# One kernel for cross attention and a mixture of experts: x's four transposes as one piece in the fourth step, and half of the projection moved behind the third step's transposes

## The reference

```
x = x + attention(layernorm(x), ctx)       # 32 batches, 112 rows of 256; ctx 375 rows of 192
    q = x @ Wq; k, v = ctx @ Wkv            # 16 heads of 64
    out = softmax(q k^T / 8) v @ Wproj + bproj
x = x + experts(layernorm(x))               # 8 experts, FF 512, the best 2 of each row, weighted
    hidden = silu(h @ gate_w_e) * (h @ up_w_e);  out_e = hidden @ down_w_e
```

## Time and profile before

| | |
|---|---|
| median of 3 runs | 1471.22 us (1470.12 to 1472.51) |
| the profiled execution | 1469.35 us, its span 1467.6 us |
| busy share of the span | PE 97%, PEld 86%, DVE 72%, ACT 58%, POOL 43% |
| granted clock of PE, mean | 0.994 |

### The profile page before, as it was taken

The page is one execution under the profiler, slowest core; times in us unless marked ns, Lnnn a source line. Parts: engine busy times, 40 slices in busy tenths (PEclk is TensorE's granted clock), DMA queues, the critical chain, the costliest instruction groups (busy, mean ns, idle before and its releaser), DMA issues.

```text
span 1467.6 us, 38599 instructions
## 1 busy us (share of the span) xinstructions
PE 1426.4 (97%) x11960; PEld 1264.4 (86%) x11961; DVE 1054.7 (72%) x2868; ACT 854.5 (58%) x2392; POOL 624.9 (43%) x671
## 2 busy tenths in 40 slices
PE   6999999999999999999999999999997999999996
PEld 5888889888888888888888898888886788888885
DVE  5667777777777777777777777777767776666664
ACT  5566556555665566656655656566555565555553
POOL 3634344344545343544344444545436243333332
PEclk9999999999999999999999999999999999999999
DMA  9322222222222232322222222212128243333232
GB/s 264 108 68 69 75 72 76 67 76 67 73 67 75 72 88 76 99 74 67 73 67 77 70 73 70 73 38 73 31 64 312 50 69 54 57 51 57 51 57 26
DMA packets 101508, 114.75 MB, mean 78 GB/s; under 512 B 17276, under 2 KB 88172, under 8 KB 101356
## 3 DMA queue, kind: packets, MB, share of 16 engines
q1 hardware_dynamic: 88300, 95.25, 22.3%
q0 software_dynamic: 12144, 15.66, 6.0%
q10 hardware_dynamic: 1024, 3.34, 0.7%
HBM read 62.28 MB, written 51.93 MB: 78 GB/s over the span
## 4 chain that ended last, share of the span: by engine, by line
PE 91%; DVE 3%; DMA 3%; issue 1%; ACT 0%; ACTq 0%; POOLq 0%; DVEq 0%; SPq 0%
PE bank L1486 26%; PE bank L1429 21%; PE bank L1555 11%; PE bank L1531 10%; PE bank L1521 9%; PE bank L1576 6%; PE bank L1493 4%; DMA out<-y_out,dest_now 2%; PE bank L1729 2%; DVE probT L1285 1%; PE bank L1682 1%; DVE Wgu L1138 1%; DMA WkU_whole<-in_L_xattn_Wkv 1%; DVE stat L1127 0%; DVE x L1125 0%
## 5 line engine op out<-in xcount | busy, mean ns | idle before, releaser
L891 ACT ACTIVATE prob<-bank,neg_max 112x375 f32<-112x375 f32 x512 | 300.4, 589 | 136.1 <-DVE neg_max L1279 136.1
L1279 DVE TENSOR_REDUCE neg_max<-bank 112x1 f32<-112x375 f32 x512 | 243.8, 539 | 16.4 <-PE bank L1521 16.3
L1531 PE MATMUL bank<-ident,prob 112*125 112x112 f32 x1536 | 213.8, 273 | 2.6 <-ACT prob L891 2.4
L1531 PEld LDWEIGHTS bank<-ident,prob 112*125 112x125 f32 x1536 | 198.3, 188 | 16.1 <-ACT prob L891 4.7
L1555 PEld LDWEIGHTS bank<-probT,V 125*64 125x64 f32 x3072 | 149.0, 137 | 39.7 <-issue 37.0
L822 POOL DMA_INDIRECT out<-y_out,dest_now x63 | 97.8, 1552 | 199.9 <-DMA out<-y_out,dest_now 139.8
L1046 DVE TENSOR_TENSOR K_l<-bank,K_h 128x376 fp32r<-128x376 f32 x256 | 140.3, 549 | 57.1 <-ACT K_h L847 52.7
L1555 PE MATMUL bank<-probT,V 125*64 125x112 f32 x3072 | 176.6, 264 | 3.3 <-DVE probT L1285 2.5
L1429 PE MATMUL bank<-Wgu,hT_h 128*128 x504 | 164.7, 408 | 3.4 <-DVE hT_l L1347 2.8
L845 ACT COPY V<-bank 125x512 f32<-125x512 f32 x96 | 56.4, 587 | 164.7 <-PE bank L1493 162.2
L847 ACT CAST K_h<-bank 128x376 fp32r<-128x376 f32 x256 | 121.0, 473 | 31.2 <-PE bank L1486 29.7
(11 more groups left out here) (217 smaller groups left out, 3962.1 us busy)
## 6 DMA issues: line engine op xcount, KB each, us to landing
bins<-pad_rows SPq DMA_DIRECT2D x29, 1032.0 KB, 6.0
inv_rows<-sums SPq DMA_DIRECT2D x126, 128.0 KB, 2.9
h_in<-bins SPq DMA_DIRECT2D x63, 129.0 KB, 2.2
Wgu<-in_L_ffn_gate_up_w SPq DMA_DIRECT2D x6, 1024.0 KB, 6.8
y_sb<-in_ctx SPq DMA_DIRECT2D x32, 187.5 KB, 2.7
y_sb<-in_ctx SPq DMA_DIRECT2D x62, 93.8 KB, 2.7
x_sb<-in_x SPq DMA_DIRECT2D x16, 224.0 KB, 2.9
x_res<-in_x SPq DMA_DIRECT2D x32, 112.0 KB, 2.5
```

The costliest lines, as they stand in the source:

```text
L891: nc.scalar.activation(prob[:, j, :], S_ps[j][0:LQ, 0:LKV], ACT.Exp, bias=neg_max[:, j:j + 1], accum_out=row_sum[:, head // HB, head % HB: ...
L1279: nc.vector.tensor_reduce(neg_max[:, j:j + 1], S_ps[j][0:LQ, 0:LKV], AX.X, ALU.max, negate=True).then_inc(max_done, 1)
L1531: last = nc.tensor.transpose(S_ps[j][0:KR, t * LQ:t * LQ + LQ], prob[:, j, t * KR:t * KR + KR], ident[0:LQ, 0:LQ])
```

## The change

`xT` becomes one piece of four transposes into one bank, in place "early" of the even batch's fourth step, with one copy by ACT and one subtraction by DVE, each of 448 columns. The pieces of the third step's "late" place go. In the fill it is one piece as well, and the banks of the pieces behind it shift by one. In even batches the projection of the batch before is cut in its two halves: the first stays where it was, the second goes behind the third step's last six transposes, and DVE's `residual` goes behind its two copies and the low part of q. Odd batches keep their projection. A wait for `x2_done` is added ahead of "early" in the fourth step.

```diff
-    one = [("q", p) for p in q_at] + {(0, 2): [("xT", 0)], (0, 3): [("xT", 1)]}.get((odd, s), [])
+    one = [("q", p) for p in q_at] + {(0, 3): [("xT", 0)]}.get((odd, s), [])
...
-    ("K", 0), ("xT", 0), ("xT", 1), ("K", 1), ("K", 2), ("K", 3), ("q", 0), ("q", 1), ("K", 4), ("K", 5), ("q", 2),
+    ("K", 0), ("xT", 0), ("K", 1), ("K", 2), ("K", 3), ("q", 0), ("q", 1), ("K", 4), ("K", 5), ("q", 2),
...
-                    nc.scalar.copy(xT_h[:, :, arg * LQ:arg * LQ + LQ],
-                                   src[:, 0:2 * LQ].rearrange("p (k q) -> p k q", k=2)).then_inc(hi_done, 1)
+                    nc.scalar.copy(xT_h[:].rearrange("p k q -> p (k q)"), src[:, 0:4 * LQ]).then_inc(hi_done, 1)
...
-                    lo, hi = xT_l[:, :, arg * LQ:arg * LQ + LQ], xT_h[:, :, arg * LQ:arg * LQ + LQ]
-                    ps = src[:, 0:2 * LQ].rearrange("p (k q) -> p k q", k=2)
+                    lo, hi = [t[:].rearrange("p k q -> p (k q)") for t in (xT_l, xT_h)]
+                    ps = src[:, 0:4 * LQ]
...
-                        if s == 2 and there(b - 1, B):
+                        if s == 2 and there(b - 1, B) and odd:
                             residual(i, b - 1, 1 - odd, A_ps[1])
                         if there(b, B):
                             turned(b, s, 0)
...
                         for k in made_at["mid"]:
                             low_part(a, k)
+                        if s == 2 and there(b - 1, B) and not odd:
+                            residual(i, b - 1, 1 - odd, A_ps[1])
...
-                    pe.wait_ge(xn_done, 2 * (0 if a.first else pair + 1) + arg + 1)
-                    for t in range(2):
-                        last = nc.tensor.transpose(dst[:, t * LQ:t * LQ + LQ], xn[:, arg, t * P:t * P + P],
-                                                   ident[0:LQ, 0:LQ])
+                    pe.wait_ge(xn_done, 2 * (0 if a.first else pair + 1) + 2)
+                    for r in range(2):
+                        for t in range(2):
+                            last = nc.tensor.transpose(dst[:, (2 * t + r) * LQ:(2 * t + r) * LQ + LQ],
+                                                       xn[:, r, t * P:t * P + P], ident[0:LQ, 0:LQ])
...
                         for k in early:
+                            if s == 3 and there(b - 1, B):
+                                pe.wait_ge(x2_done, b)
                             make(a, k, i)
                         if s == 2 and there(b - 1, B):
                             how, n = a.out(a.last_in(1, odd, 1))
                             pe.wait_ge(out_of[how], n)
-                            project(b - 1, A_ps[1])
+                            if odd:
+                                project(b - 1, A_ps[1])
+                            else:
+                                project_half(b - 1, A_ps[1], 0)
...
                         if there(b, B):
                             turn_prob(b, s, 1)
+                        if s == 2 and there(b - 1, B) and not odd:
+                            project_half(b - 1, A_ps[1], 1)
```

More of the change, by code:

```diff
@@ L667, in norm_x @@
                     a = Ahead(pair - 2 if not known(pair) or pair > 1 else None)
-                    pool.wait_ge(made, a.made(a.find(int(a.first), "xT", 1)))
+                    pool.wait_ge(made, a.made(a.find(int(a.first), "xT", 0)))
                 pool.wait_ge(rs1, pair + 1)
@@ L1444, in make @@
                 if kind == "xT":
-                    pe.wait_ge(xn_done, 2 * (0 if a.first else pair + 1) + arg + 1)
-                    for t in range(2):
-                        last = nc.tensor.transpose(dst[:, t * LQ:t * LQ + LQ], xn[:, arg, t * P:t * P + P],
-                                                   ident[0:LQ, 0:LQ])
+                    pe.wait_ge(xn_done, 2 * (0 if a.first else pair + 1) + 2)
[3 more added lines that the diff above has]
+                                                       xn[:, r, t * P:t * P + P], ident[0:LQ, 0:LQ])
                 elif kind == "q":
                     if arg == 0:
-                        pe.wait_ge(lo_done, a.split(a.find(1 if a.first else 0, "xT", 1)))
+                        pe.wait_ge(lo_done, a.split(a.find(1 if a.first else 0, "xT", 0)))
                     if a.first and arg in (0, HP // 2):
@@ L1572, in project, with project_half @@
                 for half in range(2):
[L1573 to L1577, removed]
-                last.then_inc(proj_made, 1)
+                    project_half(b, bank, half)
+            def project_half(b, bank, half):
+                pe.wait_ge(OT_lo, 2 * b + half + 1)
+                for j in range(HALF * half, HALF * half + HALF):
+                    for n, (w, m) in enumerate(((OT_h, WpH), (OT_h, WpL), (OT_l, WpH))):
+                        last = mm(bank[0:LQ, 0:C], w[:, j, :], m[:, j, :], start=j == 0 and n == 0,
+                                  stop=j == NJ - 1 and n == 2)
+                if half:
+                    last.then_inc(proj_made, 1)
             def count(b):
```

## The result

The changed kernel takes 1477.0 us in the median of 9 runs (1474.0 to 1481.6), the kernel before, beside it, 1470.1 (9 runs, 1467.8 to 1473.3): ratio 1.0045, 95% interval 1.003 to 1.006. It is slower by some 7 us; I had forecast 0.8 faster, with 0.09 on slower, and 1477.0 lies outside the range. The profiled execution took 1474.97 (span 1473.2), that of before 1469.35 (span 1467.6).

A forecast was written before the change was run, and what follows sets the result against it. PE's own stream was taken as the bound, about 90% of the chain of waits. Third step -4.2, fourth +2.8, DVE +0.3 and fill +0.3 gave -0.8 us: 1470.4 from a median of 1471.22, range 1467.4 to 1473.6.

The forecast's parts named there:

- The step that failed: GpSimd's norm_h, split_O, multiplication and scatter start 2.0 us later; 6.30 us of idle time behind them, so cost 0.
- the rule on grouping operations: Skill's rule, applied to the even fourth step: grouping pays where ScalarE or VectorE is saturated; spoke against the merged piece, 0.18 us.
- Third step: Even batch, PE: xn's transposes leave and the projection's second half comes in; -0.28 us, over 15 pairs -4.2.
- Rival C: Even third step: the wait ahead of PV stays, gain 0.18 or nothing instead of 0.28 us; 1471.9 to 1474.6; chance 0.09.
- Fourth step: Even batch: the cast of 448 columns delays head 3's exponential and PE behind it; +0.19 us, over 15 pairs +2.8.
- Rival B: Even fourth step doesn't pay for the larger cast: +0.01 instead of +0.19 us, 1467.7; chance 0.13.
- a cast saved: One ScalarE cast fewer in the even third step: worth 0.05 us of ACT, where PE does not wait for it.
- VectorE between the two: Between even third and fourth steps: residual 1.99 us later uses up the idle time before the maxima; +0.02, 14 times, +0.3.
- Rival A: DVE late at the fourth step, all four maxima move: 1472.2 at 0.15 us lateness, 1475.0 at 0.35; chance 0.18.
- The fill: Before the loop: two more of xn's transposes ahead of K on PE; +0.3 us, bounds 0 and 0.5.
- My sign of failure: Prediction wrong if a PE gap appears in an untouched step, or the fourth grows over 0.3 or under 0.1 us.

The follow-up runs named there:

- the two edits that take the two operations apart: Changed kernel, even batches: GpSimd's split_O ahead of the next mean (1469.39 us, 0.9995), or VectorE's low part of yB in the third step (1468.53 us, 0.9991).
- xT alone: Kernel before with x's transposes as one piece, projection and residual not moved: 1474.16 us, 1.0022.
- half cast: Changed kernel with ScalarE casting only 224 of the 448 columns of x's transposes in the loop: 1482.5 us in one run.
- both orders corrected: Changed kernel, even batches, with yB's low part in the third step and split_O ahead of the next mean: 1.0049 and 1.0036 on chip B, 0.9992 on C.
- yB early: Changed kernel with VectorE's low part of yB moved to the third step of even batches: 0.9991 on chip A, 0.9989 on B.
- half delay: Kernel before with two small GpSimd operations, 1.05 us together, ahead of its multiplication in even batches: 1493.0 us in one run.

## Why the prediction was wrong

**The step that failed** is the one on POOL: "norm_h, split_O, the multiplication and the scatter start 2.0 us later, with the statistics. POOL had 6.30 us of idle time behind that work, ahead of 621.81: 0." The shift was right: GpSimd's `std` went from 1.97 ahead of the fourth step's scores (605.42 to 607.39) to 0.31 behind them (611.65 to 611.96). That is 2.28, and the scores themselves are 0.30 earlier, so 1.98 later. The zero was not right. I asked only who waits for GpSimd's results and who stands behind it in its queue, and not which operations of VectorE the moved work would lie beside. The multiplication came to lie over yB's low part, and its 2.38 us cost 1.56 of VectorE, 1.03 of the maxima and 0.59 of PE in each of 14 pairs: 8.3 us. The kernel before with GpSimd alone later shows the same step, and each of the two edits that take the two operations apart brings it back to 8.32 to 8.37.

The Trainium skill states this (page SBUF — State Buffer, section Who interferes with whom): VectorE and GpSimd share a pair of SBUF ports as an exclusive lock, an operation of VectorE with two SBUF inputs contends with one of GpSimd that reads SBUF, and one with at most one SBUF input, outside the modes that use two ports, doesn't. The trace agrees for the multiplication: 2.11 for yB's low part and 2.06 for `weighed`, each to 0.3 or 0.4 behind its end. In the kernel before, the copy of probT and xT's low part, which read PSUM, took 0.50 and 0.38 within it, as elsewhere. It does not agree for every operation of GpSimd that reads SBUF: beside `hn`, which does, VectorE's `picked` with its two SBUF inputs was not held (the last section has the rows). Of the Trainium skill I had weighed the rule on grouping operations, and not the one that spoke against this change.

The rest, point by point:

- Third step: -0.30 (forecast -0.28, bounds -0.18 and -0.37). Right, and only with the move, as the run with xT alone shows. Rival C falls.
- Fourth step: +0.18 (forecast +0.19), by the larger cast ahead of head 3's exponential: 0.18 by the half cast. Twice the 0.23 of the small cast less the 0.41 of the large one leaves the 0.05 that the prediction gave for a cast saved. Rival B falls.
- VectorE between the two: the residual starts 1.97 later (forecast 1.99), and the maxima 0.80 behind the scores, 0.81 before (forecast +0.02). bin_row took 0.16. Rival A falls. Its figure of 1475.0 is the nearest to the result by luck: its lateness was to come in the fourth step, where there was none.
- The fill: K's product stood behind two transposes more, as forecast, but the first scores came at 30.8 and 32.0 in two profiles of the kernel before and at 31.9 and 33.9 in two of the changed kernel. A term of 0.3 can't be read from that; it stays open.
- My sign of failure, "if a PE gap appears in a step that the change does not touch", is what appeared.

With both orders corrected the kernel comes out at -0.9 us (interval -2.5 to +0.1) on chip C for a forecast of -0.8. That the two agree so closely is partly luck: the interval reaches past zero, and the two moves are not in the forecast. In the 14 pairs it is 966.2 to 964.8, -1.4, where the terms of the sum give 14 * (-0.28 + 0.19 + 0.02) = -1.0.

## What to carry to other kernels

When work is moved, look not only at its queue and its consumers but at what it will run beside: list VectorE's operations with two SBUF inputs that a long multiplication or subtraction of GpSimd comes to cover, and price each as held to that one's end. Such a wait is found by comparing the duration of the same form in both traces (minimum and maximum, not the mean), since no idle time stands ahead of it: for yB's low part 0.55, 0.55 and 2.13 are the least, the median and the most over the changed kernel, and 0.55 all three in the kernel before. And before a fraction of a per cent is believed, the same kernel should run on more than one chip.

## What the runs showed of the hardware

- On one of three chips, what waited for TensorE's signals started late while GpSimd's second indirect DMA ran, until 0.5 to 0.8 us behind its end: 0.9 us late for V's last product with both orders corrected, the records of PE itself undisturbed. Two of these kernels ran on another chip too, yB early on A and both orders corrected on C, and showed none of it there. By where it fell it cost from 0.2 to some 1.4 us a pair (8.50 for 8.32, and 9.72 in the one run of the half delay). Why one chip does so stays open.
- A VectorE operation of 0.55 held by GpSimd's multiplication ended up to 0.42 behind the multiplication's recorded end, not at it (619.55 and 619.97); `picked`, 0.17 us with two SBUF inputs, took 0.43 beside OT_l, in the kernel with both orders corrected:

```profile
610.92 0.43 DVE L1203 TENSOR_TENSOR picked<-onehot,bin_at 112x16 f32<-112x16 f32 x1
```

```profile
610.18 1.15 POOL L712 TENSOR_TENSOR OT_l<-O_now,OT_h 128x448 fp32r<-128x448 f32 x1
```

- Not every operation of GpSimd that reads SBUF holds such an operation. Beside `hn` (one input of 256 columns from SBUF, scaled row by row) `picked` took 0.16 to 0.19 in all 321 cases of the 18 traces, with up to 1.2 us of `hn` still to run. The kernel before has them so:

```profile
607.17 0.17 DVE L1202 TENSOR_TENSOR picked<-onehot,bin_at 112x16 f32<-112x16 f32 x1
```

```profile
606.51 2.43 POOL L753 TENSOR_SCALAR hn<-x,mv,std 112x256 f32<-112x256 f32 x2 [0.20 <-POOL std L747]
```

- `bin_row`, also with two SBUF inputs, took 0.32 to 0.37 instead of 0.16 beside `hn` where it started 0.19 to 0.44 us into one of its two operations, and 0.16 where it started 1.03 or more into it. That is the 0.33 of the odd batches in the earlier trace rows: up to 0.2 us more, and not a wait to the end of `hn`. What sets these cases apart from the multiplication no run shows.
